# A four-block graph network on one core: transfers ordered by stream, an empty instruction as holder of TensorE's waits, and new stage orders

## The chip, the cores and the metric

The kernel runs on one core of one Trainium2 chip. The metric is the device time of one execution in microseconds, the median of a few runs. The text uses the names of the profile for the engines: PE (TensorE), DVE (VectorE), ACT (ScalarE), POOL (GpSimd) and SP (SyncE, which here does nothing but wait and issue transfers); PEld is the loading of weights into PE.

## The reference, cut to what matters

128 graphs of 64 nodes with 384 features pass four blocks. Each block takes h = relu(layernorm(x)), computes f(h) and adds it to x, all in float32.

```python
h = jnp.maximum(_layernorm(x, axis=-1), 0.0)
x = x + _L0_gnn_ref(h, adj, ...)      # two layers, attention from two projections of h
h = jnp.maximum(_layernorm(x, axis=-1), 0.0)
x = x + _L1_gnn_ref(h, adj, adj, ...) # 12-head attention, bias adj + adj
h = jnp.maximum(_layernorm(x, axis=-1), 0.0)
x = x + _L2_gnn_ref(h, adj, ...)      # 12-head attention, bias adj
h = jnp.maximum(_layernorm(x, axis=-1), 0.0)
x = x + _L3_gnn_ref(h, adj, ...)      # two layers, upper, diagonal and lower part apart
```

One layer of the first block, and of the last:

```python
u = u_left * adj_tri + u_left * diag_mask + u_right * jnp.swapaxes(adj_tri, 1, 2)
delta_exp_u = jnp.exp(u) * adj
attention = delta_exp_u / (jnp.sum(delta_exp_u, axis=2, keepdims=True) + 1e-10)
ctx = jnp.matmul(attention, h @ W_lin.T + b_lin)
h = jax.nn.relu(_layer_norm(ctx, ln_a[l], ln_b[l]))
...
ctx = jnp.einsum('bij,bjd->bid', attn * upper, hl) + diag_a[..., None] * hs + jnp.einsum('bij,bjd->bid', attn * lower, hr)
```

## The kernel before, in words

**Tiles.** A group is 4 graphs, 256 rows of x, held as 128 partitions by 2 by 384. There are 32 groups. They are dealt to two streams, 0 and 1, with buffers and four PSUM banks each; a stream does 16 groups (ITER) per block. The blocks (phases) run one after the other with a barrier between them: phase 0 is the first block, phases 1 and 2 are the attention blocks, phase 3 the last. x goes to memory between phases.

**Products.** A projection is done as three matmuls on a high and a low part (`exact_product`, L161 to L163). `ml`, `mr` and `lin` are the three projections of a layer in phase 0, `w0`, `w1`, `w2` those in phase 3, `q`, `k`, `v`, `out` those of attention. PE's transposes (`hT`, `pt`, `aT`) and the small products (`u` or `scores`, `agg` or `pv`) stand between them.

**Order.** Each phase has four lists of words, one for each of PE, ACT, DVE and POOL (`GCN0_ORDERS`, `ATT_ORDERS`, `GCN3_ORDERS`). A word such as `agg_0.1` is a stage, its layer and its stream; a prime means that the stage works in round r on group r-1. `run_stages` issues the list once a round, rounds 2 to 15 as a loop. Each engine goes through its list in that order and waits where a count of another engine is not yet reached; nothing overtakes. So a list fixes what stands behind a stage that waits.

**A group's way.** SP brings x (`xin`) and the adjacency (`adjin`); DVE takes row statistics (`stat`), POOL makes scale and shift of them (`stat` on POOL, four small operations, one of them a power), ACT makes h (`norm`, L432, L828, L1230), PE transposes it (`hT`), ACT and DVE split it in high and low part (`t_lo` is the last), and the projections follow. In a layer, `ea` is the masked exponential, `aT` its transpose, `lin` or `w2` on DVE the evacuation of a projection with its bias, which `agg` on PE reads. In attention, DVE's `soft` and `fac` give a factor by which POOL's `p` scales the exponentials (three pieces p0, p1, p2), PE transposes them (`pt0` to `pt2`), ACT evacuates (`pT`), PE multiplies by v (`pv0` to `pv2`).

**Transfers.** SP's program is `move_program`. In a round it waits and issues for stream 0 and stream 1 the loads of group i, and then for stream 0 and stream 1 the stores of group i-1 (with `x_again`, a second load of x for the residual, in phases 0 and 3). A load waits until the buffers are free: `adjin` by a stage of POOL, `xin` by ACT's `norm`. A store waits for DVE's `xout`. SP is one queue too: a load behind a store waits for that store's wait.

**A small matmul that waits.** Before `agg` and `pv`, PE issues `take_wait` (L121): a product of the identity with one column, into a corner of a PSUM bank that nobody reads. The waits of the stage are on it, and the tiled matmuls after it wait for nothing.

Of the kernel before, what the change touches and what calls it, by code (L numbers as in the profile page):

```python
# [12 lines left out]
STREAMS = 2  # L13
GROUPS = GRAPHS * NODES // TOK
ITER = GROUPS // STREAMS
HEADS = 12
HD = FEAT // HEADS
HT = HEADS * T
HPC = P // HD
BANK = 512  # L20
# [8 lines left out]
GCN0_ORDERS = [  # L29
# [10 lines left out]
]  # L40
PT_BANK = (0, 2, 3)
ATT_ORDERS = [
# [6 lines left out]
]  # L49
GCN3_ORDERS = [  # L50
# [13 lines left out]
]  # L64
# [53 lines left out]

def take_wait(nc, g, b, bank=1):

    nc.tensor.matmul(b.ps[0:HD, bank, BANK - 1:BANK], g.ident[:, 0:HD], g.ident[:, 0:1], start=True, stop=True)  # L121

# [82 lines left out]
def move_program(nc, sp, g, phase, n_mats, rows, x_out, bufs, sems, adj_free, x_free, x_new,  # L205
                 x_again=None):
# [15 lines left out]
    def store(s, i):  # L222
        x_new(s, i)
        sp.dma_start(x_out[i * STREAMS + s], bufs[s].xout[:]).then_inc(sems.stored[s], 16)
# [17 lines left out]

    def turn(i):
        for s in range(STREAMS):
            load(s, i, i - 1)
        for s in range(STREAMS):
            store(s, i - 1)
            if x_again:
                x_again(s, i)
    turn(1)  # L250
    with sp.Fori(2, ITER) as i:
        turn(i)
    if phase + 1 < len(g.sources):
        for s in range(STREAMS):
            sp.wait_ge(sems.stored[s], 16 * (ITER - 1) + 1)
            load(s, 0, ITER - 1, of=phase + 1)
    for s in range(STREAMS):
        store(s, ITER - 1)
    for s in range(STREAMS):
# [28 lines left out]
def gcn0_phase(nc, g, phase, x_out, b_lin, gain, beta, ln_cols):  # L288
# [20 lines left out]
    with ExitStack() as ctx:  # L309
        def sb(name, shape, dt=F32):  # L310
            return ctx.enter_context(nc.sbuf_tensor(f"{name}_{phase}", shape, dt))
        sems = phase_sems(nc, g, ctx, phase)
# [8 lines left out]
        for s in range(STREAMS):  # L321
            b = Buf()
# [291 lines left out]
        def _(pe):  # L614
            pe.wait_ge(g.const_in, g.const_count)

            def layer(l):
# [62 lines left out]
                def agg(s, i):  # L680
                    b = bufs[s]

                    pe.wait_ge(dve_done[s], DV[s](f"lin_{l}", i))
                    pe.wait_ge(act_done[s], AC[s](f"aT_{l}", i))
                    take_wait(nc, g, b, 2 * l + 1)
                    for half in range(2):
# [13 lines left out]
def attention_phase(nc, g, phase, bias_times, x_out, bv, bo):  # L700
# [13 lines left out]
    with ExitStack() as ctx:  # L714
        def sb(name, shape, dt=F32):
            return ctx.enter_context(nc.sbuf_tensor(f"{name}_{phase}", shape, dt))
        sems = phase_sems(nc, g, ctx, phase)
# [5 lines left out]
        for s in range(STREAMS):  # L723
            b = Buf()
# [231 lines left out]
        def _(pe):  # L956
# [66 lines left out]
            def pv(c):  # L1023
                def stage(s, i):
                    b = bufs[s]
                    pe.wait_ge(act_done[s], AC[s](f"pt{c}", i))
                    take_wait(nc, g, b)
                    for t in range(T):
# [29 lines left out]
def gcn3_phase(nc, g, phase, x_out, w_rows, gain, beta, ln_cols):  # L1058
# [19 lines left out]
    with ExitStack() as ctx:  # L1078
# [353 lines left out]
        def _(pe):  # L1432
            pe.wait_ge(g.const_in, g.const_count)

            def layer(l):
# [61 lines left out]
                def agg(s, i):  # L1497
# [3 lines left out]
                    pe.wait_ge(pool_done[s], PO[s](f"w0_{l}", i))  # L1501
                    take_wait(nc, g, b, 3)
                    for k, m in enumerate((UPPER, LOWER)):
# [128 lines left out]
```

## Time and profile before

| | |
|---|---|
| median of three runs | 3173.35 us (3173.3 to 3178.01) |
| the profiled execution, its own time | 3173.94 us |
| its span, first to last instruction | 3172.1 us |
| PE busy | 2881.0 us, 91% |
| DVE, POOL, ACT busy | 2047.8, 1251.3, 1215.9 us |
| transfers | 158.83 MB, mean 50 GB/s |

The profiled execution lies 0.6 us above the median, and 1.8 us of its time are outside the span. In the profile a line of a view is a group of instructions or a stretch of time; "idle ... <- X" is time in which the engine had nothing running, with the instruction whose end released it.
### The profile page before, as it was taken

Reading aid. Unit: us, or ns where it says so; the run is one execution under the profiler, and the core shown is the slowest. Engines: PE = TensorE matmul, PEld = TensorE weight load, DVE = VectorE, ACT = ScalarE, POOL = GpSimd, SP = SyncE. Lnnn points to the kernel's source line nnn. Section 1 sums busy time; section 2 is a strip of 40 time slices with the busy share of each in tenths; the row PEclk is TensorE's granted clock in tenths of the full one; section 3 lists DMA queues with packets and bytes.
Section 4 is the critical chain, followed back from the end, with each engine's and each line's share of the span. In section 5 each row is a group of like instructions: output and inputs, shape, how many; then the busy total and the mean of one; then the engine's idle time right before and its main releaser. Section 6 shows DMA issues by size and latency. Waiting matters only on the chain. (4 is left out here: it accounts for less than half of the span.)

```text
span 3172.1 us, 83110 instructions
## 1 busy us (share of the span) xinstructions
PE 2881.0 (91%) x33408; PEld 2633.1 (83%) x33408; DVE 2047.8 (65%) x3932; ACT 1215.9 (38%) x1941; POOL 1251.3 (39%) x2315
## 2 busy tenths in 40 slices
PE   6999999999978999999969999999699999999997
PEld 6888888888877888888858888888588888888886
DVE  4655665656665777777657777777566666666666
ACT  3333333333333333333333333333344444444443
POOL 2111211212113333333323333333267777676767
PEclk9999999999999999999989999999799999999999
DMA  3111111111111111111111111111201010111010
GB/s 132 48 54 45 46 63 45 38 63 46 63 47 59 44 43 43 43 44 44 47 57 45 43 48 43 43 43 43 74 14 67 33 66 33 66 33 66 33 65 31
DMA packets 116483, 158.83 MB, mean 50 GB/s; under 512 B 8000, under 2 KB 112320, under 8 KB 116416
## 3 DMA queue, kind: packets, MB, share of 16 engines
q1 hardware_dynamic: 116416, 157.88, 15.2%
q8 instruction: 49, 0.80, 0.1%
q14 instruction: 18, 0.15, 0.0%
HBM read 107.52 MB, written 50.33 MB: 50 GB/s over the span
## 5 line engine op out<-in xcount | busy, mean ns | idle before, releaser
L161 PE MATMUL ps<-t_hi,w_hi 128*128 128x256 f32 x2304 | 669.6, 291 | 44.9 <-DVE t_lo L898 42.3
L162 PE MATMUL ps<-t_lo,w_hi 128*128 128x256 f32 x2304 | 652.6, 283 | 0.0
L163 PE MATMUL ps<-t_hi,w_lo 128*128 128x256 f32 x2304 | 651.7, 283 | 0.0
L161 PE MATMUL ps<-w_hi,t_hi 128*128 128x384 f32 x1536 | 532.9, 347 | 16.2 <-DVE t_lo L1348 12.4
L163 PE MATMUL ps<-w_hi,t_lo 128*128 128x384 f32 x1536 | 518.1, 337 | 0.0
L162 PE MATMUL ps<-w_lo,t_hi 128*128 128x384 f32 x1536 | 518.0, 337 | 0.0
L161 PEld LDWEIGHTS ps<-t_hi,w_hi 128*128 128x128 f32 x2304 | 442.8, 192 | 75.3 <-DVE t_lo L898 52.1
L812 POOL TENSOR_TENSOR e<-e,factor 128x512 f32<-128x512 f32 x192 | 195.3, 1046 | 762.9 <-DVE factor L936 762.9
L162 PEld LDWEIGHTS ps<-t_lo,w_hi 128*128 128x128 f32 x2304 | 442.8, 192 | 0.0
L163 PEld LDWEIGHTS ps<-t_hi,w_lo 128*128 128x128 f32 x2304 | 441.6, 192 | 0.0
L161 PEld LDWEIGHTS ps<-w_hi,t_hi 128*128 128x128 f32 x1536 | 288.4, 188 | 28.6 <-DVE t_lo L1348 14.4
L1194 POOL TENSOR_TENSOR hw<-hw,w_row 128x192 f32<-128x192 f32 x512 | 294.7, 610 | 39.2 <-ACT hw L1275 39.0
L162 PEld LDWEIGHTS ps<-w_lo,t_hi 128*128 128x128 f32 x1536 | 288.9, 188 | 0.0
L163 PEld LDWEIGHTS ps<-w_hi,t_lo 128*128 128x128 f32 x1536 | 288.4, 188 | 0.0
L415 POOL TENSOR_TENSOR rstd<-mv,pos_half 128x2 f32<-128x2 f32 x64 | 44.1, 690 | 577.8 <-DVE mv L592 577.8
L942 DVE TENSOR_TENSOR o_lo<-ps,o_hi 128x768 fp32r<-128x768 f32 x64 | 61.3, 958 | 294.9 <-ACT o_hi L867 294.9
L848 ACT ACTIVATE k<-ps 128x768 f32<-128x768 f32 x64 | 52.0, 813 | 397.5 <-PE ps L163 397.5
L1275 ACT ACTIVATE hw<-ps 128x768 f32<-128x768 f32 x128 | 103.6, 810 | 205.4 <-PE ps L163 205.4
L843 ACT ACTIVATE q<-ps 128x768 f32<-128x768 f32 x64 | 52.1, 814 | 291.0 <-PE ps L163 291.0
L804 POOL TENSOR_TENSOR xout<-xin,bo_row 128x192 f32<-128x192 f32 x256 | 143.7, 595 | 0.0
L161 PE MATMUL ps<-w_hi,o_hi 128*128 128x384 f32 x384 | 131.9, 343 | 4.7 <-DVE o_lo L942 4.7
L161 PE MATMUL ps<-w_hi,swap_hi 128*128 128x384 f32 x384 | 134.4, 350 | 0.0
(152 smaller groups left out, 6165.6 us busy)
## 6 DMA issues: line engine op xcount, KB each, us to landing
x_after<-xout SPq DMA_DIRECT2D x96, 384.0 KB, 2.5
xin<-x_after SPq DMA_DIRECT2D x96, 384.0 KB, 3.4
xin<-in_x SPq DMA_DIRECT2D x32, 384.0 KB, 4.7
x<-in_x SPq DMA_DIRECT2D x32, 384.0 KB, 3.6
x<-x_after SPq DMA_DIRECT2D x32, 384.0 KB, 4.2
out<-xout SPq DMA_DIRECT2D x32, 384.0 KB, 3.0
w_raw<-in_w SPq DMA_DIRECT2D x4, 2304.0 KB, 9.3
adjin<-in_adj SPq DMA_DIRECT2D x32, 256.0 KB, 4.3
```

The source lines that it names most:

```text
L161: nc.tensor.matmul(out, lhs_hi, rhs_hi, start=(k == 0), stop=False)
L162: nc.tensor.matmul(out, lhs_hi, rhs_lo, start=False, stop=False)
L163: last = nc.tensor.matmul(out, lhs_lo, rhs_hi, start=False, stop=(k == len(terms) - 1))
L415: nc.gpsimd.tensor_tensor(b.rstd[:], b.mv[:, :, 1], g.pos_half[:, 0:T], ALU.pow).then_inc(pool_done[s], 1)
L804: ins = nc.gpsimd.tensor_tensor(b.xout[:, rows, at], b.xin[:, rows, at], bo_row[:, at], ALU.add)
L812: nc.gpsimd.tensor_tensor(b.e_rows[:, c * n:(c + 1) * n], b.e_rows[:, c * n:(c + 1) * n], b.factor[:, c * n:(c + 1) * n].unsqueeze(2).broa ...
L843: nc.scalar.activation(b.q[:], b.ps_row, ACT.Copy).then_inc(act_done[s], 1)
L848: nc.scalar.activation(b.k[:], b.ps_row2, ACT.Copy).then_inc(act_done[s], 1)
L942: nc.vector.tensor_tensor(b.o_lo_by_graph, b.ps_o, b.o_hi_by_graph.bitcast(F32), ALU.subtract)\
L1194: ins = nc.gpsimd.tensor_tensor(b.hw[:, rows, m, at], b.hw[:, rows, m, at], w_row[l][m][:, at], ALU.add)
L1275: nc.scalar.activation(b.hw[:, :, m], b.ps_w[m], ACT.Copy).then_inc(act_done[s], 1)
```

## The change

Three things are changed; what is computed is the same.

1. `move_program`: the loop goes by stream. For each stream it stores group i-2, loads x again for group i-1, and loads group i. At the end of a phase the first load of the next phase stands by its stream, and waits for one store less.
2. `take_wait` with its matmul becomes `take_waits`, which issues `nop` on PE. In the built program it is a bare wait of PE's sequencer; no matmul stands there.
3. All twelve orders are new. In phases 0 and 3 they also start at another place of the cycle, so that other stages carry the prime.

```diff
-def take_wait(nc, g, b, bank=1):
-
-    nc.tensor.matmul(b.ps[0:HD, bank, BANK - 1:BANK], g.ident[:, 0:HD], g.ident[:, 0:1], start=True, stop=True)
+def take_waits(pe):
+
+    pe.nop(nofuse=True)
...
-    def turn(i):
+    def store_and_reload(s, i):
+        store(s, i)
+        if x_again and (not isinstance(i, int) or i + 1 < ITER):
+            x_again(s, i + 1)
+    for s in range(STREAMS):
+        load(s, 1, 0)
+    with sp.Fori(2, ITER) as i:
         for s in range(STREAMS):
+            store_and_reload(s, i - 2)
             load(s, i, i - 1)
-        for s in range(STREAMS):
-            store(s, i - 1)
-            if x_again:
-                x_again(s, i)
-    turn(1)
-    with sp.Fori(2, ITER) as i:
-        turn(i)
-    if phase + 1 < len(g.sources):
-        for s in range(STREAMS):
-            sp.wait_ge(sems.stored[s], 16 * (ITER - 1) + 1)
+    for s in range(STREAMS):
+        store_and_reload(s, ITER - 2)
+        if phase + 1 < len(g.sources):
+            sp.wait_ge(sems.stored[s], 16 * (ITER - 2) + 1)
             load(s, 0, ITER - 1, of=phase + 1)
     for s in range(STREAMS):
-        store(s, ITER - 1)
+        store_and_reload(s, ITER - 1)
...
-                    take_wait(nc, g, b, 2 * l + 1)
+                    take_waits(pe)
```

Of the orders, PE's list of phase 0 and DVE's of attention:

```diff
-    "ml_1.0' agg_0.1' mr_1.0' u_1.0' hT_1.1' lin_1.0' aT_1.0' mr_1.1' agg_1.0' hT_0.0 ml_1.1' ml_0.0 "
-    "mr_0.0 u_1.1' lin_1.1' aT_1.1' u_0.0 hT_0.1 lin_0.0 aT_0.0 agg_1.1' agg_0.0 ml_0.1 mr_0.1 hT_1.0 "
-    "u_0.1 lin_0.1 aT_0.1",
+    "aT_1.0' mr_1.1' hT_0.0 agg_1.0' u_1.1' lin_1.1' mr_0.0 aT_1.1' ml_0.0 hT_0.1 u_0.0 lin_0.0 aT_0.0 "
+    "agg_1.1' agg_0.0 ml_0.1 mr_0.1 hT_1.0 u_0.1 lin_0.1 aT_0.1 agg_0.1 ml_1.0 mr_1.0 hT_1.1 lin_1.0 "
+    "u_1.0 ml_1.1",
...
-    "stat.0 pv.0' hT.0 soft.1' out.0' fac.1' v.0 stat.1 pv.1' hT.1 soft.0 out.1' fac.0 v.1",
+    "stat.0 pv.0' hT.0 soft.1' out.0' stat.1 fac.1' v.0 pv.1' hT.1 soft.0 out.1' fac.0 v.1",
```

**SP in the loop of phase 0.** The rows are in order of issue; the number at the end of `xin0`, `xout0_0` is the stream. Before:

```order
30 L216 DMA adjin0<-in_adj 128x512
31 L361 ISA
32 L220 ISA
33 L220 DMA xin0<-in_x 128x2x384
34 L358 ISA
35 L216 ISA
36 L216 DMA adjin1<-in_adj 128x512
37 L361 REGISTER_ALU
38 L220 ISA
39 L220 DMA xin1<-in_x 128x2x384
40 L364 ISA
41 L224 ISA
```

The stores (L224) come behind both loads, and the next round's loads behind both stores. Now:

```order
26 L225 DMA x_after_0<-xout0_0 128x2x384
27 L369 ISA
28 L369 DMA x0_0<-in_x 128x2x384
29 L360 ISA
30 L217 ISA
31 L217 DMA adjin0<-in_adj 128x512
32 L363 REGISTER_ALU
33 L221 ISA
34 L221 DMA xin0<-in_x 128x2x384
35 L366 REGISTER_ALU
36 L225 ISA
37 L225 DMA x_after_0<-xout1_0 128x2x384
```

The load of stream 0 now stands right behind the store of stream 0, and ahead of that of stream 1.

**DVE in the loop of attention, stream 1's softmax.** `sum`, `rsum`, `factor` are the stage `fac`; `x_st1`, `x_mv1` are stream 1's row statistics. Before:

```order
343 L949 TENSOR_TENSOR xout0_1<-ps0,xout0_1 128x768
344 L930 REGISTER_ALU
345 L931 TENSOR_REDUCE sum1_1<-e1_1 128x24
346 L879 REGISTER_ALU
347 L933 RECIPROCAL rsum1_1<-sum1_1 128x24
348 L879 REGISTER_ALU
349 L936 SCALAR_TENSOR_TENSOR factor1_1<-absmax1_1,rsum1_1 128x24
350 L906 REGISTER_ALU
351 L907 TENSOR_TENSOR v0_1<-ps0,bv_row_1 128x768
352 L885 BN_STATS x_st1_1<-xin1 128x6 x2
353 L888 MEMSET pad 128x1
354 L890 BN_AGGR x_mv1_1<-x_st1_1 128x2 x2
```

Now:

```order
341 L951 TENSOR_TENSOR xout0_1<-ps0,xout0_1 128x768
342 L887 BN_STATS x_st1_1<-xin1 128x6 x2
343 L881 REGISTER_ALU
344 L890 MEMSET pad 128x1
345 L892 BN_AGGR x_mv1_1<-x_st1_1 128x2 x2
346 L932 REGISTER_ALU
347 L933 TENSOR_REDUCE sum1_1<-e1_1 128x24
348 L881 REGISTER_ALU
349 L935 RECIPROCAL rsum1_1<-sum1_1 128x24
350 L938 SCALAR_TENSOR_TENSOR factor1_1<-absmax1_1,rsum1_1 128x24
```

The statistics of stream 1 moved ahead of the factor. On ACT `norm.1` moved with them, from behind the evacuations `pt0.1'` to `pt2.1'` to ahead of `k.0`; stream 0's stages kept their places on both engines but for `pt2.0'`, which now goes before `pt1.0'`.

## Rows read from the trace of the kernel before

**Rows 1.** The page: the span, and each engine's busy time.

```profile
span 3172.1 us, 83110 instructions
PE 2881.0 (91%) x33408; PEld 2633.1 (83%) x33408; DVE 2047.8 (65%) x3932; ACT 1215.9 (38%) x1941; POOL 1251.3 (39%) x2315
```

**Rows 2.** Windows: us, busy time by engine, granted clock; two rounds of phase 0.

```profile
523.20:581.50 58.30, 54.30 (x454) 49.30 (x453) 34.37 (x88) 19.34 (x37) 10.53 (x24) 0.97 0.15 49
...
637.40:693.30 55.90, 52.79 (x454) 47.79 (x453) 34.38 (x88) 19.30 (x37) 10.53 (x24) 1.00 0.16 52
```

**Rows 3.** PE's waits, 118 to 918 us (phase 0): total, times, longest.

```profile
PE ps L668 <- ACT mlr L465: 16.0, 28, 0.9
PE ps L627 <- ACT h L432: 15.1, 14, 1.1
PE ps L121 <- DVE hw L553: 13.1, 14, 1.6
PE ps L677 <- DVE ea L571: 3.8, 14, 0.3
```

**Rows 4.** The same, 1020 to 1560 us (phase 1).

```profile
PE ps L965 <- ACT h L828: 22.0, 27, 1.4
PE ps L161 <- DVE t_lo L898: 16.1, 27, 0.7
```

**Rows 5.** The same, 2390 to 3120 us (phase 3).

```profile
PE ps L161 <- DVE t_lo L1348: 11.5, 13, 0.9
PE ps L121 <- DVE aT L1392: 7.7, 13, 0.6
PE ps L1447 <- ACT h L1230: 6.1, 12, 0.9
```

**Rows 6.** Timeline of SP and DVE, phase 0: start, us, what, idle before.

```profile
521.75 0.40 SPq L224 DMA_DIRECT2D x_after<-xout  x1
...
523.84 0.37 SPq L220 DMA_DIRECT2D xin<-in_x  x1
...
528.87 1.02 DVE L503 BATCH_NORM_STATS2 x_st<-xin 128x6 f32<-128x384 f32 x2 [2.77 <-DMA xin<-in_x]
```

**Rows 7.** Timeline of PE, phase 0: a round's cluster of waits, and one in its end.

```profile
531.15 0.22 PE L121 MATMUL ps<-ident 128*32 128x1 f32 x2 [1.45 <-DVE hw L553]
...
533.25 1.24 PE L627 MATMUL ps<-ident,h 128*128 128x128 f32 x6 [1.07 <-ACT h L432]
...
937.06 0.22 PE L121 MATMUL ps<-ident 128*32 128x1 f32 x2 [0.94 <-DVE hw L553]
```

**Rows 8.** Timeline of SP and DVE in phase 1.

```profile
1299.53 0.40 SPq L220 DMA_DIRECT2D xin<-x_after  x1
...
1302.90 1.02 DVE L885 BATCH_NORM_STATS2 x_st<-xin 128x6 f32<-128x384 f32 x2 [2.06 <-DMA xin<-x_after]
```

**Rows 9.** Timeline of PE, ACT and POOL in phase 1, stream 0's half.

```profile
1300.05 3.05 POOL L812 TENSOR_TENSOR e<-e,factor 128x512 f32<-128x512 f32 x3 [12.15 <-DVE factor L936]
...
1302.74 1.47 PE L1019 MATMUL ps<-ident,e 128*128 128x128 f32 x12
...
1303.64 1.57 ACT L859 ACTIVATE pT<-ps 128x512 f32<-128x512 f32 x3
1305.84 1.30 ACT L828 ACTIVATE h<-xin,x_shift,x_rstd 128x384 f32<-128x384 f32 x2 [0.62 <-POOL x_shift L786]
...
1304.82 0.22 PE L121 MATMUL ps<-ident 128*32 128x1 f32 x2
1304.98 0.45 PE L1033 MATMUL ps<-pT,v 64*32 64x64 f32 x32
...
1307.20 0.88 PE L965 MATMUL ps<-ident,h 128*128 128x128 f32 x6 [1.23 <-ACT h L828]
```

**Rows 10.** Lines: the waiting matmul's group; PEld behind a wait held by a register instruction.

```profile
L121 PE MATMUL ps<-ident 128*32 128x1 f32 x640 | 71.3, 181 | 30.9 <-DVE hw L553 15.0 <-DVE aT L1392 9.3 <-DVE hw L1357 1.0
...
1308.00 0.62 PEld L1007 LDWEIGHTS ps<-k,q 32*64 32x64 f32 x49 [0.17 <-issue]
```

More of the change, by code:

```diff
@@ L1026, in stage @@
                     pe.wait_ge(act_done[s], AC[s](f"pt{c}", i))
-                    take_wait(nc, g, b)
+                    take_waits(pe)
                     for t in range(T):
@@ L1501, in agg @@
                     pe.wait_ge(pool_done[s], PO[s](f"w0_{l}", i))
-                    take_wait(nc, g, b, 3)
+                    take_waits(pe)
                     for k, m in enumerate((UPPER, LOWER)):
```

51 rows, old and new, of tables (ATT_ORDERS, GCN0_ORDERS, GCN3_ORDERS) are left out of this document.

## The prediction, made before the changed kernel ran

> **What bounds the kernel now.** The page comes first: PE is busy 2881.0 of 3172.1 us, DVE as the next only 2047.8 [rows 1]. So an edit is worth what it takes out of PE's queue or out of its waits. Next I read PE's waits phase by phase, in stretches of whole rounds away from the phase ends. Phase 0: 48.0 us in 14 rounds, 3.4 a round [rows 3]. Phase 1: 38.1 us in 13.7 rounds of 39.4 us, 2.8 a round [rows 4], and phase 2 has the same program. Phase 3: 25.3 us in 13.5 rounds of 54.2 us, 1.9 a round [rows 5]. Together they are some 160 us, and that is about what orders can win. The releasers are always the last link of a chain over DVE and ACT (t_lo, h, mlr, hw).
>
> Two things in the windows and timelines make some of these waits longer than the chain needs.
>
> First, x comes late. In phase 0 SP issues the load of stream 0 at 523.84, after the store of stream 1 at 521.75, and DVE, whose `stat.0` stands ahead of `lin_1.1'`, sits idle 2.77 us for it [rows 6]. Behind that `stat` PE waits 1.45 us for hw and then 1.07 us for h [rows 7]. In phase 1 the same load is issued at 1299.53 and DVE idles 2.06 us [rows 8]; h then starts 0.6 us after ACT's last pT [rows 9] and PE waits 1.23 us for it, against 0.48 us in stream 1's half.
>
> Second, the clock. A round of phase 0 takes 58.3 us at granted clock 0.97, with PE busy 54.30 us, and 55.9 us at 1.00, with 52.79 us for the same 454 matmuls [rows 2]. In the first, after the 1.45 and 1.07 us of waiting, the transpose takes 1.24 us [rows 7]: PE fell from 2.4 to 1.2 GHz there. Of the 14 rounds 8 are of that kind.
>
> **The transfers.** In SP's new loop the load of stream 0 stands behind the store of stream 0 alone. In phase 0 that store is issued half a round before stream 1's, and the load then waits for POOL to have read `adjin`, which happens before stream 1's xout in the new order too. So x is there some 10 us or more before `stat.0`, and the 2.77 us are gone. Stream 1's load is queued behind the wait for stream 1's xout as before, but its `stat` stands later behind that point on all lists. The extra queueing (a store now waits behind the other stream's load) costs nothing: the load's waits end before the xout it stands ahead of. In phase 1 the load can go when POOL's `xb.0` and `bias.0` are done, 10 us before 1299.53.
>
> **Attention, per round.** Stream 0's half: x no longer late, DVE's `stat.0` ends about 1302.2 rather than 1304.2. POOL finishes p at 1303.10 (1300.05 plus 3.05), its four stat operations take about 1.6 us, so shift is there at 1304.7 and h can start when ACT has done the third pT, at 1305.2, rather than at 1305.84 [rows 9]. That is 0.6 us. Stream 1's half: `norm.1` leaves the place behind pT, so h (1.30 us) is off the chain and the transpose can follow `pv2` at once. But `stat.1` now delays the factor by 1.02 plus 0.33 us. POOL's pieces come at 1.02 us each; PE had 1.6 us of slack on p0 (1301.1 against 1302.74 [rows 9]), and the third piece will now be some 0.65 us late. And what is late next is o_hi on ACT and t_lo on DVE, which start only 0.2 to 0.3 us earlier. I take 0.2 us. Together 0.8 us a round, times 15 rounds, times 2 phases: **24 us**. If the third piece is later than I think, stream 1's half loses 0.4 us instead: 0.2 us a round is the low end, 6 us.
>
> **Phase 0, per round.** I followed PE's new list through the round with the durations of the rows and these gaps between engines, stage by stage. The h wait (1.07) and the hw wait of `agg_1.1'` (0.55 to 1.45) go, as `stat.0` and `lin_1.1'` lie well ahead of their readers. `u_1.1'` gets `hT_0.0` and `agg_1.0'` ahead of it and finds mlr ready, and `u_1.0` has `lin_1.0` ahead. That takes the 0.9 us one away. What stays or comes: `u_0.0` and `u_0.1` have only one transpose between them and the projection that they need, which shows as 0.24 us each in rounds of before (28 waits hold 16.0 us, in pairs of 0.90 and 0.24 [rows 3]). And `agg_0.1` now stands right behind `aT_0.1` and `lin_0.1`, without `ml_1.0` between them: it waits for DVE to evacuate hw. The trace has that very sequence in the tail of the phase: 0.94 us [rows 7]. With 0.1 us for a tight `aT_0.0` that is 1.5 us in place of 3.4. So 1.9 us a round.
>
> **The empty instruction.** The small matmul comes 320 times (640 records, two each [rows 10]). From its start to the first tiled matmul go 0.16 us (1304.82 to 1304.98 [rows 9]), 51 us in all. In attention the first two of three stand in a stretch that ACT's pT sets (three in 1.57 us, and PE's three repeat at the same 0.53 us), so only the last counts, and I have it in the 0.2 us. In phases 0 and 3 there are four a round on PE's path. No row shows a bare wait ahead of these tiles. The nearest is the wait that a register instruction holds ahead of `scores`: PEld pauses 0.17 us there [rows 10] while PE runs on. So each stop is worth between +0.16 (all of it) and -0.17 us (the pause falls on PE too). Most waits of `agg` are over before PE arrives, so I take the near side: 0.1 us, 0.4 us a round.
>
> The Trainium skill ("PSUM — Partial Sum Buffer", Engine vs sequencer instructions) counts a nop among the instructions that the sequencer runs itself, while weight loads overlap running matmuls inside the engine. By that rule the tiles' weight loads could not be taken up before the wait ends. No row shows it for `agg`; it is the low side of the bound above, and the sum stands without it.
>
> Phase 0 is then 2.3 us times 15 rounds, 35 us. The cluster of waits that came before the fall of the clock is gone, so I count the 1.5 us of 8 rounds too: 12 us. **47 us**.
>
> **Phase 3, per round.** h loses its late x, `w0` gets other work ahead, and aT's evacuation too. By the walk `agg_0.0` and `agg_0.1` wait for DVE's w2, which stands behind splits and `stat`-like work: 0.5 us each as a gap, about 0.35 as the profile counts it. So 0.7 in place of 1.9 us; with the empty instruction 1.2 plus 0.4, times 15: **24 us**. One place could fail here: `adj_1.1'` is now primed, so stream 1's load goes out only in the new round. It should land 2 us before `stat.1` wants it.
>
> **Phase ends.** The tails hold the same stages as before in nearly the same order, and at the start of a phase x was there already; I count 0.
>
> **Sum.** 24 + 47 + 24 = 95 us off 3173.9, the execution's own time: **3079 us**, and 3078 for a median such as that shown.
>
> **The rivals.**
>
> *Only the transfers pay.* The walk fixes no wait that I didn't look for; DVE runs in order, and one stage placed ahead of its input gives each gain back. Then what stays is what the late x cost: 0.6 us in 30 attention rounds (18), about 1.0 us in 15 rounds of phase 0 (15), the clock (12), and 0.4 in phase 3 (6): 51 us, 3123. For it: the new order of phase 0 has slack below 1 us at four places. Against it: I found those slacks positive. If the loads, against what SP's list says, still come late because POOL frees `adjin` late, it is the reverse: 95 less 45, 3129.
>
> *More than the sum.* Attention also ran below full clock (0.98 on average in phase 1); without falls there and with the full 0.16 us for the stops: another 15 and 10 us, 3054.
>
> *The bare wait costs.* At -0.17 us on all 320 stops the sum loses 54 us and the 12 counted: 3145. By the page's rule above it would go that way.
>
> *Slower: the clock.* The new 0.94 us wait with short ones about it could put PE at 1.2 GHz in every round, where now most of the run is at 2.4. At 1.5 us a fall, once a round in phases 0 and 3 (32) and once in each half round of attention (64): 144 us, plus the 12 counted, from 3079: 3235. It decides the sign from 63 falls on. For it: rows 2 show falls after waits. Against: they came where two waits of over 1 us lay 2 us apart [rows 7], and no such pair is left; attention with waits of 1.23 us has few falls.
>
> **How the numbers follow.** Forecast 0.58 (3055 to 3105); only the transfers, or the loads late, 0.19 (3123, 3129); more than the sum 0.12 (3054 and less); the bare wait 0.06 (3145); slower 0.05 (3235). I choose the range 3040 to 3132: it leaves out the last two cases and the far end of the third. What a measurement can tell from no change is about 0.2%, 6 us. Faster by more than that 0.93, within it 0.02, slower 0.05.
>
> **What would show it.** In the changed profile: no DVE idle on `xin` in the rounds; SP's load of stream 0 alone, far from stream 1's; h waits of PE near 0.6 us in one half of attention and near none in the other; one hw wait of about 0.9 us a round in phase 0; rounds of about 53.8, 38.5 and 52.6 us in the three kinds of phase; granted clock 1.00 in nearly all of phase 0. The forecast is wrong if `stat.1` ahead of `fac.1'` makes PE wait for POOL's e by more than 1 us, if `agg` and `pv` start late behind their bare waits, or if new waits of over 1 us stand close together.

## The result, and the profile after

| | before | changed |
|---|---|---|
| median of four runs, same chip | 3175.68 us (3173.3 to 3179.95) | 3056.23 us (3054.35 to 3056.87) |
| ratio, 95% interval | | 0.9621 (0.9605 to 0.9638) |
| the profiled execution, its own time | 3173.94 us | 3056.15 us |
| its span | 3172.1 us | 3054.4 us |

The change takes 117.7 us off the span where 95 were forecast. The page of the changed kernel, in the form of [rows 1]; its third line is the granted clock in 40 slices, in tenths:

```profile
span 3054.4 us, 82121 instructions
PE 2807.4 (92%) x32768; PEld 2576.5 (84%) x32768; DVE 2043.4 (67%) x3932; ACT 1214.8 (40%) x1941; POOL 1311.5 (43%) x2315
...
PEclk9999999999989999999989999999799999999999
```

PE still sets the time. Its busy time fell by 73.6 us and its idle time (span less busy) by 44.1 us, from 291.1 to 247.0. Of the busy time 46.9 us went with the 640 small matmuls and 26.7 us from matmuls that both kernels have; the run with transfers and orders alone, below, parts the two.

The four phases of both kernels follow, each row from the start of a phase to the start of the next: length, busy time of PE, PEld, DVE, ACT and POOL with counts, granted clock, share of the DMA engines, GB/s. First before:

```profile
0.00:948.60 948.60, 860.97 (x7232) 780.49 (x7232) 557.16 (x1416) 317.40 (x584) 172.29 (x394) 0.98 0.17 57
948.60:1613.10 664.50, 593.09 (x9792) 559.10 (x9792) 449.98 (x518) 239.72 (x325) 224.81 (x386) 0.96 0.14 46
1613.10:2272.60 659.50, 585.71 (x9792) 552.54 (x9792) 449.22 (x518) 239.71 (x325) 224.77 (x385) 0.97 0.15 46
2272.60:3172.10 899.50, 841.26 (x6592) 740.98 (x6592) 591.41 (x1480) 419.03 (x710) 629.40 (x1152) 0.98 0.15 49
```

And the changed kernel:

```profile
0.00:894.70 894.70, 829.33 (x7104) 756.37 (x7104) 547.04 (x1419) 315.61 (x584) 189.94 (x394) 0.99 0.18 61
894.70:1539.30 644.60, 575.79 (x9600) 543.14 (x9600) 445.72 (x521) 241.98 (x325) 224.14 (x386) 0.98 0.15 47
1539.30:2183.80 644.50, 577.40 (x9600) 544.51 (x9600) 445.75 (x518) 241.80 (x325) 224.03 (x385) 0.97 0.15 47
2183.80:3054.40 870.60, 824.85 (x6464) 732.51 (x6464) 604.88 (x1480) 415.38 (x710) 673.43 (x1152) 0.98 0.16 50
```

The gains are 53.9, 19.9, 15.0 and 28.9 us; the forecast had 47, 12, 12 and 24. A round of phase 0 in the form of [rows 2], and one of phase 3:

```profile
474.27:527.77 53.50, 51.56 (x446) 47.05 (x445) 33.67 (x89) 19.22 (x36) 11.80 (x24) 1.00 0.16 54
...
2381.61:2433.94 52.33, 51.25 (x406) 45.50 (x405) 37.50 (x93) 25.57 (x45) 42.14 (x73) 1.00 0.16 50
```

PE's waits (total, times, longest) in phase 0, 110 to 900 us, in the form of [rows 3]:

```profile
PE ps L692 <- DVE hw L555: 17.4, 15, 1.5
PE ps L692 <- DVE asum L578: 4.4, 14, 0.3
PE ps L670 <- ACT mlr L467: 3.4, 14, 0.2
PE ps L670 <- ACT mlr L462: 3.4, 14, 0.2
```

in phase 1, 920 to 1514 us, in the form of [rows 4]:

```profile
PE ps L162 <- DVE t_lo L900: 23.0, 30, 0.8
PE ps L1035 <- ACT pT L861: 8.4, 17, 0.5
PE ps L1021 <- POOL e L814: 6.3, 17, 0.9
PE ps L967 <- ACT h L830: 3.6, 15, 0.2
```

and in phase 3, 2250 to 3000 us, all that is left of the kinds of [rows 5]:

```profile
PE ps L1510 <- DVE hw L1359: 14.7, 29, 0.7
```

SP in phase 0, where [rows 6] had the load of stream 0 2.1 us behind the store of stream 1. Now the load of stream 0 stands 17.8 us ahead of that store (493.95), and no round shows DVE idle on `xin`:

```profile
474.27 0.40 SPq L225 DMA_DIRECT2D x_after<-xout  x1
...
476.14 0.38 SPq L221 DMA_DIRECT2D xin<-in_x  x1
493.95 0.40 SPq L225 DMA_DIRECT2D x_after<-xout  x1
```

### The profile page after: what moved, and what is told of

Read it like the earlier page. It is cut to its first block and busy times, and to the rows that moved or that the text cites. A ratio compares the mean times of both kernels' runs of the same rounds, so it can differ in the third digit from the quotient of the medians.

```text
span 3054.4 us, 82121 instructions
## 1 busy us (share of the span) xinstructions
PE 2807.4 (92%) x32768; PEld 2576.5 (84%) x32768; DVE 2043.4 (67%) x3932; ACT 1214.8 (40%) x1941; POOL 1311.5 (43%) x2315
## 5 line engine op out<-in xcount | busy, mean ns | idle before, releaser
L162 PE MATMUL ps<-t_hi,w_hi 128*128 128x256 f32 x2304 | 662.7, 288 | 51.7 <-DVE t_lo L900 49.1
L1196 POOL TENSOR_TENSOR hw<-hw,w_row 128x192 f32<-128x192 f32 x512 | 348.1, 711 | 53.8 <-ACT hw L1277 52.3
L417 POOL TENSOR_TENSOR rstd<-mv,pos_half 128x2 f32<-128x2 f32 x64 | 53.4, 835 | 459.9 <-DVE mv L594 459.9
L781 POOL TENSOR_TENSOR x_shift<-x_mv,neg_one 128x2 f32<-128x2 f32 x64 | 14.3, 224 | 351.0 <-DVE x_mv L892 351.0
L544 DVE CAST t_hi<-hT 128x768 fp32r<-128x768 f32 x64 | 35.7, 558 | 191.6 <-ACT hT L446 137.2
```

Source lines behind the costliest of these rows:

```text
L162: nc.tensor.matmul(out, lhs_hi, rhs_hi, start=(k == 0), stop=False)
L417: nc.gpsimd.tensor_tensor(b.rstd[:], b.mv[:, :, 1], g.pos_half[:, 0:T], ALU.pow).then_inc(pool_done[s], 1)
L1196: ins = nc.gpsimd.tensor_tensor(b.hw[:, rows, m, at], b.hw[:, rows, m, at], w_row[l][m][:, at], ALU.add)
```

## The experiments

The theory is that of the prediction: the loads come in time, the orders take waits away, and each stop is a little shorter. The rivals are that the transfers alone pay, that a bare wait costs, and that the orders are worth something without the early loads. Each of the three parts was made alone and with each other one; four runs then undo or alter single moves, one sizes the stop, and one repeats the changed kernel. None leaves out any part of the reference. A ratio stands against runs of the kernel before on the same chip beside it. Spans and phases are of one profiled execution each.

| | median us | ratio (95%) | span | phase 0, 1, 2, 3 |
|---|---|---|---|---|
| before | | | 3172.1 | 948.6, 664.5, 659.5, 899.5 |
| transfers alone | 3097.23 | 0.9779 (0.9763 to 0.9796) | 3094.2 | 905.0, 649.2, 649.2, 890.8 |
| stops alone | 3158.86 | 0.9971 (0.996 to 0.9981) | 3154.1 | 938.0, 661.7, 659.5, 894.9 |
| orders alone | 3260.94 | 1.0294 (1.0277 to 1.0311) | 3259.8 | 985.9, 664.2, 662.7, 947.0 |
| transfers and orders | 3082.34 | 0.9732 (0.9716 to 0.9749) | 3080.9 | 900.4, 651.0, 652.0, 877.5 |
| orders and stops | 3247.33 | 1.0251 (1.0221 to 1.028) | 3247.1 | 982.7, 658.4, 656.9, 949.1 |
| transfers and stops | 3084.66 | 0.972 (0.9699 to 0.9741) | 3083.3 | 898.5, 649.0, 651.2, 884.6 |
| all three | 3056.23 | 0.9621 (0.9605 to 0.9638) | 3054.4 | 894.7, 644.6, 644.5, 870.6 |

The kernel before took 3163.1 to 3180.0 us over all its executions, so a span set against its 3172.1 is less sure than the ratio. By the medians on one chip the transfers alone are worth 71.6 us (77.9 by span), the stops alone 9.9 (18.0), and the orders alone cost 92.2 (87.7). With the new transfers the repeats of a kernel lie within 6 us of each other.

### Transfers alone (e1_transfers)

The kernel before with the new SP loop:

```diff
-    def turn(i):
-        for s in range(STREAMS):
-            load(s, i, i - 1)
-        for s in range(STREAMS):
-            store(s, i - 1)
...
+    with sp.Fori(2, ITER) as i:
+        for s in range(STREAMS):
+            store_and_reload(s, i - 2)
+            load(s, i, i - 1)
```

> The kernel before with the new transfer program alone; old orders and the small waiting matmul stay. Theory (late x costs waits and, through them, clock): DVE's idle of 2.8 us on xin in phase 0 is gone, h comes earlier in phase 0 and in stream 0's half of attention, and the falls of the clock in phase 0 go. 51 us off 3175.7, so about 3125 (3110 to 3145). Rival (the orders carry the gain, x could be late without cost): at most 10 us off, 3166 or more.

Measured: 3097.23 us, faster than the expected range. That is 71.6 us by the medians and 77.9 us off the span, where I had sized 51. The phases of this kernel:

```profile
0.00:905.00 905.00, 845.68 (x7232) 767.13 (x7232) 556.44 (x1416) 317.15 (x584) 170.84 (x394) 1.00 0.18 60
905.00:1554.20 649.20, 583.99 (x9792) 551.43 (x9792) 447.83 (x519) 237.95 (x325) 223.86 (x386) 0.98 0.15 47
1554.20:2203.40 649.20, 584.73 (x9792) 552.13 (x9792) 447.70 (x519) 237.84 (x325) 223.77 (x385) 0.98 0.15 47
2203.40:3094.20 890.80, 840.07 (x6592) 742.96 (x6592) 590.56 (x1480) 418.15 (x710) 631.43 (x1152) 0.98 0.15 49
```

and PE's waits in phase 0, 25 to 880 us:

```profile
PE ps L669 <- ACT mlr L466: 19.2, 33, 0.9
...
PE ps L121 <- DVE hw L554: 0.9, 1, 0.9
```

In phase 0 both kinds of wait that follow stream 0's `stat` are gone, h and hw, 28.2 us in 14 rounds [rows 3], not the h wait alone. The idle time falls from 87.6 to 59.3 us and, for the same 7232 matmuls, the busy time from 860.97 to 845.68 at a granted clock of 1.00 for 0.98. Over the four phases 51.3 us are idle time and 26.6 us busy time.

### The empty instruction alone (e2_nop)

```diff
-    nc.tensor.matmul(b.ps[0:HD, bank, BANK - 1:BANK], g.ident[:, 0:HD], g.ident[:, 0:1], start=True, stop=True)
+    pe.nop(nofuse=True)
```

> The kernel before with the empty instruction alone in place of the small waiting matmul. Theory (each stop saves 0.06 us where its wait ends last and 0.15 us where it is over already): 10 to 20 us off, about 3160 (3153 to 3168). Rival (a bare wait holds back the weight loads and costs about what the matmul cost): 3176, up to 3230 at 0.17 us lost per stop.

Measured: 0.9971, 9.9 us between the medians, the low end of the 10 to 20 expected. The two profiled spans lie 18.0 us apart, 10.6 of it in phase 0 and 4.6 in phase 3. In these two executions the small matmuls' own busy time goes (43.2 us), and 25.2 us come back as idle time: where the stop waits for something, shortening it only starts the wait earlier. A bare wait does not cost, so that rival falls.

### The orders alone (e3_orders), and orders and empty instruction on the old transfers (e5_old_transfers)

The first is the kernel before with all twelve new lists, of which PE's list of phase 0 shows the kind:

```diff
-    "ml_1.0' agg_0.1' mr_1.0' u_1.0' hT_1.1' lin_1.0' aT_1.0' mr_1.1' agg_1.0' hT_0.0 ml_1.1' ml_0.0 "
+    "aT_1.0' mr_1.1' hT_0.0 agg_1.0' u_1.1' lin_1.1' mr_0.0 aT_1.1' ml_0.0 hT_0.1 u_0.0 lin_0.0 aT_0.0 "
```

> The kernel before with the new orders alone; old transfers and the small waiting matmul stay. Theory (the new orders take stat.0 soon after stream 1's xout, and count on x being there): stream 0's x lands 7 us after the store of stream 1, DVE stands still for some 5 us a round, PE's h wait grows by 3 to 4 us a round in phases 0 and 3 and 0.6 in attention; nothing is left of the gain: about 3186 (3160 to 3210). Rival (the three parts add up, and the orders carry most): 3115 or less.

The second is the changed kernel with the old SP loop:

```diff
-            store_and_reload(s, i - 2)
...
+        for s in range(STREAMS):
+            store(s, i - 1)
+            if x_again:
+                x_again(s, i)
+    turn(1)
```

> The changed kernel with the old transfer program. Theory (new orders need the early x): DVE stands still on xin for several us a round, and PE's wait for h comes to 3 us or more a round in phases 0 and 3: about 3170 (3145 to 3195). Rival (transfers and orders add up, transfers 51 us): 3107.

Measured: 3260.94 and 3247.33 us, both slower than the kernel before, some 75 us above the theory's value for each and above both ranges. Phases 0 and 3 of the second, and its waits there (25 to 958 and 2323 to 3222 us):

```profile
0.00:982.70 982.70, 862.16 (x7104) 775.42 (x7104) 549.61 (x1417) 318.19 (x584) 189.58 (x394) 0.96 0.17 55
...
2298.00:3247.10 949.10, 852.55 (x6464) 762.87 (x6464) 592.87 (x1480) 412.23 (x710) 670.20 (x1152) 0.94 0.15 46
```

```profile
PE ps L628 <- ACT h L433: 54.9, 14, 5.6
```

```profile
PE ps L162 <- DVE t_lo L1349: 51.4, 14, 4.2
```

and, in the timeline of a round of phase 0, the statistics with the idle time ahead of them and the transpose of h behind:

```profile
604.86 1.02 DVE L504 BATCH_NORM_STATS2 x_st<-xin 128x6 f32<-128x384 f32 x2 [3.71 <-DMA xin<-in_x]
...
609.14 1.37 PE L628 MATMUL ps<-ident,h 128*128 128x128 f32 x6 [3.46 <-ACT h L433]
610.44 1.56 PE L691 MATMUL ps<-hw,aT 64*64 64x384 f32 x8
```

The wait is of the size that I had given, 3.9 us a round in phase 0 (54.9 by 14). What the expectation lacked is the clock. After the wait the transposes take 1.37 us and the tiles of `agg` 1.56 us; in the changed kernel they take 0.82 and 0.88 us. Against the changed kernel, with the same 7104 and 6464 matmuls, PE is busy 32.8 us longer in phase 0 and 27.7 us in phase 3, 60.5 us of the 77 that the value for the second was off. The new orders place `hT_0.0` and what follows it early in the round. With the old loads they are not a small gain but a loss of 87.7 us of span.

### Transfers and orders, with the small matmul (e4_no_nop)

```diff
-                    take_waits(pe)
+                    take_wait(nc, g, b, 2 * l + 1)
```

> The changed kernel with the small waiting matmul put back. Theory: 15 us slower than the changed kernel, about 3071 (3064 to 3078). Rival (bare waits cost as much as the matmul): 3056 or less.

Measured: 3082.34 us, above the 3064 to 3078 expected. The empty instruction is worth 26.5 us in the changed kernel, not 12: 5.7 in phase 0 and 6.9 in phase 3, as counted (6 each), but also 6.4 and 7.5 in the two attention phases, where I had given it nothing of its own. This kernel has the 33,408 matmuls of the kernel before, so the two compare phase by phase:

```profile
0.00:900.40 900.40, 840.12 (x7232) 765.30 (x7232) 546.69 (x1416) 316.43 (x584) 190.39 (x394) 0.99 0.18 60
900.40:1551.40 651.00, 591.14 (x9792) 553.07 (x9792) 444.60 (x519) 243.24 (x325) 224.04 (x386) 0.97 0.14 47
1551.40:2203.40 652.00, 588.11 (x9792) 550.19 (x9792) 444.43 (x521) 243.45 (x325) 223.94 (x386) 0.98 0.15 47
2203.40:3080.90 877.50, 834.97 (x6592) 738.92 (x6592) 607.62 (x1480) 415.33 (x710) 672.37 (x1152) 0.98 0.16 50
```

The stop itself, in the same sequence with nothing to wait for. First this kernel, then the changed one:

```profile
503.98 0.82 PE L629 MATMUL ps<-ident,h 128*128 128x128 f32 x6
504.73 0.22 PE L122 MATMUL ps<-ident 128*32 128x1 f32 x2
504.88 0.55 PE L692 MATMUL ps<-hw,aT 64*64 64x384 f32 x4
```

```profile
500.87 0.82 PE L629 MATMUL ps<-ident,h 128*128 128x128 f32 x6
501.62 0.55 PE L692 MATMUL ps<-hw,aT 64*64 64x384 f32 x4
```

From the transposes to the first tile it is 0.90 us with the small matmul and 0.75 without: the stop costs nothing that can be seen. And where hw is late, first before, then changed:

```profile
643.43 0.93 DVE L553 TENSOR_TENSOR hw<-ps,lin_row 128x768 f32<-128x768 f32 x1
...
644.49 0.22 PE L121 MATMUL ps<-ident 128*32 128x1 f32 x2 [0.55 <-DVE hw L553]
644.63 0.55 PE L690 MATMUL ps<-hw,aT 64*64 64x384 f32 x4
```

```profile
480.42 0.96 DVE L555 TENSOR_TENSOR hw<-ps,lin_row 128x768 f32<-128x768 f32 x1 [0.16 <-PE ps L164]
...
481.63 0.88 PE L692 MATMUL ps<-hw,aT 64*64 64x384 f32 x8 [1.14 <-DVE hw L555]
```

From hw's end to the first tile it is 0.27 us (644.36 to 644.63) and 0.25 us (481.38 to 481.63). The stop is worth 0.15 us where PE comes late and 0.02 us where PE waits.

The Trainium skill ("PSUM — Partial Sum Buffer", Engine vs sequencer instructions) has the nop run by the sequencer, with weight loads overlapping inside the engine. The low side of my bound, tiles held up by 0.17 us [rows 10], to which that would fit, is not seen in these rows.

### Transfers and empty instruction, old orders (e9_old_orders)

The changed kernel with the twelve lists of before; DVE's list of attention:

```diff
-    "stat.0 pv.0' hT.0 soft.1' out.0' stat.1 fac.1' v.0 pv.1' hT.1 soft.0 out.1' fac.0 v.1",
+    "stat.0 pv.0' hT.0 soft.1' out.0' fac.1' v.0 stat.1 pv.1' hT.1 soft.0 out.1' fac.0 v.1",
```

> The changed kernel with all old orders (new transfers and the empty instruction stay). Theory (given early x and bare waits, the new orders are worth 1.2 us a round in phase 3, some 0.7 in phase 0, little in attention): about 3083 (3075 to 3090), 25 to 30 us behind the changed kernel. Rival (the orders alone carry as much as the transfers): 3110 or more.

Measured: 3084.66 us, as expected. With the early loads in place the orders alone bring 13.3 us of span, the empty instruction alone 10.9, and both 39.8. The surplus is 15.6 us (13.5 us by the medians), and attention has all of it, 15.7 us: there the one alone changes a phase by +0.2 and -2.0 us, the other by -1.8 and -2.8 (both lose a little or nothing), and together they give 4.6 and 4.7. PE's waits in phase 1, first with the transfers alone (930 to 1529 us), then with the empty instruction too (923 to 1522 us):

```profile
PE ps L966 <- ACT h L829: 14.4, 30, 0.5
```

```profile
PE ps L966 <- ACT h L829: 21.2, 31, 2.1
...
PE ps L1034 <- ACT pT L860: 5.1, 30, 0.2
```

With the old orders h comes behind the last pT on ACT. PE's shorter stops are paid back at the h wait (14.4 to 21.2 us) and at pT (5.1 us, new). In the new orders `norm.1` has left that place, the h wait is 3.6 us, and the shorter stop reaches the end of the round. What is late next is t_lo, at 23.0 us.

### Two small matmuls for one (e10_two_matmuls)

Transfers and orders, and in `take_wait`:

```diff
-    nc.tensor.matmul(b.ps[0:HD, bank, BANK - 1:BANK], g.ident[:, 0:HD], g.ident[:, 0:1], start=True, stop=True)
+    for _ in range(2):
+        nc.tensor.matmul(b.ps[0:HD, bank, BANK - 1:BANK], g.ident[:, 0:HD], g.ident[:, 0:1], start=True, stop=True)
```

> The changed kernel with two small matmuls in a row at each of the 320 stops instead of the empty instruction. Theory (a small matmul costs 0.15 us on PE where its wait is over, and delays what waits for the tiles where it isn't): the second costs as much as the first, so some 26 us more than the kernel with one, about 3108 (3100 to 3120). Rival (the first cost something that is not its run time, such as held back weight loads): 3085.

Measured: 3094.49 us, 11.6 us of span over the kernel with one; half of what the theory gave, below its range and above the rival's 3085. A row shows why:

```profile
505.21 0.29 PE L123 MATMUL ps<-ident 128*32 128x1 f32 x4
505.43 0.55 PE L693 MATMUL ps<-hw,aT 64*64 64x384 f32 x4
```

From the stop to the first tile it is 0.22 us, 0.07 more than with one. The first small matmul costs twice the second. The 26.5 us of the empty instruction are thus 320 stops at 0.08 us each, and a second small matmul adds 0.04. How the tiles would do with their waits on themselves, with no holder at all, was not tried and stays open.

### agg_0.1 moved back behind ml_1.0 (e7_agg_back)

```diff
-    "agg_1.1' agg_0.0 ml_0.1 mr_0.1 hT_1.0 u_0.1 lin_0.1 aT_0.1 agg_0.1 ml_1.0 mr_1.0 hT_1.1 lin_1.0 "
+    "agg_1.1' agg_0.0 ml_0.1 mr_0.1 hT_1.0 u_0.1 lin_0.1 aT_0.1 ml_1.0 agg_0.1 mr_1.0 hT_1.1 lin_1.0 "
```

> The changed kernel with agg_0.1 moved back behind ml_1.0 on PE in phase 0, so that DVE's hw is ready when PE comes to it. Theory (the 1.1 us wait is the price for n_0.1 in time for hT_1.1; moved back, hT_1.1 waits 1.8 us instead): 0.5 us a round slower, about 3065 (3058 to 3074). Rival (the wait is a plain loss): 1.1 us a round less, 3038.

Measured: 3072.56 us, within the range but at twice the price that I had given, phase 0 912.3 for 894.7 us. PE's costliest wait in phase 0, 25 to 887 us:

```profile
PE ps L629 <- DVE z L606: 30.4, 16, 2.0
```

The 1.16 us that PE waits for hw in each round (17.4 by 15) is a price paid on purpose. With `ml_1.0` in between, that wait is gone, and the transposes of layer 1, whose input is the output of this very `agg`, come 1.9 us late instead (30.4 by 16). Filling the hw wait loses 17.6 us in the phase, 1.1 us a round where 0.5 was expected.

### The moves in attention (e8_stat1_back, e6_att_old, e11_pt_in_order)

First the changed kernel with `stat.1` and `norm.1` where they stood before:

```diff
-    "exp.0' k.1' pt0.0' pt2.0' pt1.0' norm.0 pv.0' hT.0 q.0 exp.1' norm.1 k.0 pt0.1' pt1.1' pt2.1' pv.1' "
+    "exp.0' k.1' pt0.0' pt2.0' pt1.0' norm.0 pv.0' hT.0 q.0 exp.1' k.0 pt0.1' pt1.1' pt2.1' norm.1 pv.1' "
...
-    "stat.0 xb.1' bias.1' stat.1 p.1' xb.0 bias.0 p.0",
+    "stat.0 xb.1' bias.1' p.1' stat.1 xb.0 bias.0 p.0",
```

> The changed kernel with stream 1's statistics and norm back behind its factor in attention (DVE, POOL and ACT), nothing else. Theory (0.2 to 0.3 us a round of stream 1's half came from this move): 6 to 9 us slower than the changed kernel, 3064 (3058 to 3070). Rival (stat.1 ahead of the factor makes p late and costs what it gives): 3056 or less.

Then the changed kernel with all four old lists of attention, among them:

```diff
-    "k.1' pt0.0' pt2.0' pt1.0' pv0.0' pv1.0' pv2.0' hT.0 scores.1' q.0 out.0' v.0 k.0 pt0.1' pt1.1' "
-    "pt2.1' pv0.1' pv1.1' pv2.1' hT.1 scores.0 q.1 out.1' v.1",
+    "v.1' k.1' pt0.0' pt1.0' pt2.0' pv0.0' pv1.0' pv2.0' hT.0 scores.1' q.0 out.0' v.0 k.0 pt0.1' pt1.1' "
+    "pt2.1' pv0.1' pv1.1' pv2.1' hT.1 scores.0 q.1 out.1'",
```

> The changed kernel with the old orders in attention alone. Theory (in attention the early x gave 0.6 us a round by itself, the orders the rest of 1.1 us): 12 us slower than the changed kernel, about 3068 (3062 to 3076). Rival (there the orders did nothing, or all): 3056, or 3090.

And the changed kernel with only the swap of stream 0's pieces taken back, on PE and ACT:

```diff
-    "k.1' pt0.0' pt2.0' pt1.0' pv0.0' pv1.0' pv2.0' hT.0 scores.1' q.0 out.0' v.0 k.0 pt0.1' pt1.1' "
+    "k.1' pt0.0' pt1.0' pt2.0' pv0.0' pv1.0' pv2.0' hT.0 scores.1' q.0 out.0' v.0 k.0 pt0.1' pt1.1' "
```

> The changed kernel with stream 0's transposes pt0, pt1, pt2 in number order again on PE and ACT. Theory (POOL's three pieces are ready, h ends last after pv): within 3 us of the changed kernel. Rival (pv1 ready early lets pv follow piece by piece, 0.1 us a round and more): 3 to 8 us faster.

| | median us | ratio (95%) | span | phase 0, 1, 2, 3 |
|---|---|---|---|---|
| stat.1 and norm.1 back | 3068.06 | 0.9684 (0.9663 to 0.9705) | 3065.9 | 894.5, 651.3, 648.8, 871.3 |
| all attention orders old | 3061.26 | 0.9663 (0.9643 to 0.9684) | 3060.0 | 895.1, 647.9, 650.3, 866.7 |
| pieces in order | 3054.54 | 0.9632 (0.9611 to 0.9653) | 3052.0 | 894.4, 642.0, 644.7, 870.9 |

Moving the two stages back costs 11.0 us in the two attention phases, and the old lists altogether 9.1. So the whole gain of the new attention orders is in that one move. By the medians the old lists cost only 5.0 us, below the 12 of the theory and just outside its range, and the one move back 11.8: without that move the other new places in the lists gain nothing and may lose. PE's waits with it undone, phase 1, 920 to 1521 us:

```profile
PE ps L967 <- ACT h L830: 15.1, 31, 2.1
PE ps L1035 <- ACT pT L861: 10.8, 31, 0.5
```

The h wait is back at 15.1 us for 3.6, while pT and e fall a little (11.6 us for 14.7 in sum). The swap of the pieces is worth nothing: the kernel without it differs from the changed one by 1.7 us with overlapping intervals. It is no better version, and none of the others beats the changed kernel. With all attention orders old phase 3 is 3.9 us shorter, though its lists weren't touched. Two of its rounds take 104.2 us (from one store of SP to another, 2443.13 to 2547.32), for 104.7 in the changed kernel (2433.94 to 2538.60), and why stays open. So a difference of some 4 us in a phase need not come from the lists of that phase.

### The changed kernel again (e12_changed_again)

No line is edited.

> The changed kernel once more, beside the other three on one chip, as their base: 3050 to 3058.

Measured: 3056.72 us, ratio 0.9636 (0.9617 to 0.9656), phases 894.9, 644.1, 645.3 and 871.1 us. The repeat is within 0.8 us in each phase.

## Why the prediction was right, and where its sum was off

The sign and the range were right, and so was the mechanism in the main: early loads, fewer waits, cheaper stops. The time was 23 us lower than forecast, and the parts did not share the gain as the walk had it. Because transfers and orders with the small matmul keep all matmuls of the kernel before, the 117.7 us fall into three parts that answer to the parts of the sum: idle time between the two (291.1 to 226.6), busy time of the same matmuls (2881.0 to 2854.3), and the empty instruction on top.

| term | forecast us | measured us |
|---|---|---|
| waits of PE, phase 0 | 28 (1.9 a round) | 27.3 |
| waits, attention | 24 | 11.5 + 9.9 |
| waits, phase 3 | 18 (1.2 a round) | 15.7 |
| empty instruction | 12 (phases 0 and 3 alone) | 26.5 (5.7, 6.4, 7.5, 6.9) |
| busy time of the same matmuls, phase 0 (forecast as clock) | 12 | 20.9, of which 15.3 with the transfers alone |
| the same, other phases | 0 | 5.8 (1.9, -2.4, 6.3) |

**The waits of PE held.** Phase 0, stage by stage: one hw wait a round, foretold 0.94 from the tail of the phase, came at 1.16 (17.4 by 15); the pair of 0.24 at u came at 0.24 each (3.4 by 14, twice); the tight `aT_0.0` foretold at 0.1 is the asum wait of 0.31. These make 1.95 us a round for the 1.5 foretold; the 27.3 us of the table are measured with the small matmul in place, where no asum wait shows. A round lasts 53.5 us in phase 0, 38.2 in attention (one of SP's stores of phase 1 to the next, 1004.38 to 1042.58) and 52.3 in phase 3, for 53.8, 38.5 and 52.6 foretold. In attention the h wait fell to 0.24 us in one half and to none in the other, where 0.6 and near none were foretold. In phase 3 the two agg waits are 0.51 each (14.7 by 29), for 0.35 foretold. All three sums are within 3 us. Of the signs that would have spoken against the forecast none came: the longest wait for POOL's e is 0.9 us, and the bare waits start nothing late. "What is late next is o_hi on ACT and t_lo on DVE" named the right limit: t_lo went from 18.1 us (31 waits, before, 974 to 1588 us) to 23.0.

**The empty instruction was mis-sized.** The step that failed is "only the last counts, and I have it in the 0.2 us": it gave the stops of attention nothing of their own, and they brought 13.9 us. The reason given, that two of the three stand in a stretch set by ACT's pT, held for the old orders, where the empty instruction alone changes attention by next to nothing. It fails once h is off the chain.

**The clock came as sized; more busy time went than the clock's.** Before, the 8 rounds at 0.97 (117.8 to 581.5 us) hold 434.5 us of busy time, and the next 5 at 1.00 hold 264.0, or 52.8 a round: 12.1 us for the clock, as "I count the 1.5 us of 8 rounds too: 12 us" had it. With the transfers alone the whole phase gives 15.3. The other 5.6 of the 20.9 came with the new orders, at a granted clock no higher: three rounds of the same matmuls take 158.0 us of busy time with the transfers alone (386.99 to 549.43) and 157.1 with the orders too (389.18 to 551.00), all at 1.00. The forecast had no term for that, and in phase 3, at 0.98 in all three, it is 5.1 of the 6.3 us. Why the busy time falls there was not tested. In attention I had kept 15 us for the rival; busy time gave 10.1 with the transfers alone (9.1 and 1.0), and next to none with the orders beside them (1.9 and -2.4).

**The transfers carry most of it.** Alone they give 77.9 us of span, 71.6 by the medians, of which the rival "only the transfers pay" had priced 51. Its weak term was "about 1.0 us in 15 rounds of phase 0 (15)": it gave the late x the h wait alone, while my own reading had said that hw stood behind the same `stat`. The idle time of the phase fell by 28.3 us. The orders and the empty instruction then brought 39.8 us on top, for the 44 that the forecast had beyond the transfers. In phase 0 the new orders do not even lower PE's waits below those of the transfers alone. From the transfers alone to transfers and orders its idle time there goes from 59.3 to 60.3 us. The mlr waits fall from 19.2 to 8.1 us and the hw waits rise from 0.9 to 17.2 (25 to 875 us), and the orders are worth 4.6 us, all of it busy time. So the 28 us of waits came out right, but not for the reason that the walk gave: it credited a good part to the new places in the lists, and the early loads alone brought it. In phase 3 both had a part: 7.5 us of idle time went with the transfers and 8.2 more with the orders.

**Which case came.** The measured time lies nearer to the 3054 of "more than the sum" than to 3079. That case had its parts half right: the stops brought more, in attention as well; attention at full clock did not come (0.98 and 0.97 over its two phases). The stops and the busy time brought more than was counted and the waits a little less; together that makes the 23 us. One sum of the prediction is wrong as it stands: "95 less 45" is 50 us, which gives 3124 and not 3129. The case "slower by the clock" did not come in the changed kernel, but its mechanism did in the runs with the old transfers: waits of 3.3 to 5.6 us in each round, and PE busy 60.5 us longer for the same matmuls in phases 0 and 3. So single waits bring falls too when they are that long; the new hw waits of 1.16 us, one a round, left phase 0 at 0.99. The z wait in the run with `agg_0.1` moved back did not bring it down either: from 160 us on that wait is 1.9 to 2.0 us in each of 14 rounds, the six transposes behind it take 0.87 or 0.88 us, and the granted clock of that stretch is 1.00 (160 to 887 us). The kernel before fell after 1.45 and 1.07 us close together [rows 7], so a wait's length alone does not tell.

## What to carry to other kernels

Where engines run fixed lists, look at the transfer queue first: new lists that placed x's consumers early lost some 90 us with the old queue, and gained 13 with the new one, so neither can be judged alone. A shortened step that is not the last link of a chain shows nothing until that link is moved, so try the two together before dropping one as useless. And a wait of 1 us in a tight loop may be the price for a longer one later; move it alone and see before filling it.

## What the runs showed of the hardware

- A bare wait of PE's sequencer ahead of tiled matmuls delays nothing that can be seen: 0.25 us from the end of DVE's write to the first tile, 0.27 us with a small matmul as holder; 0.75 and 0.90 us from the transposes ahead when nothing is waited for.
- The first small matmul of a stop takes 0.15 us of PE's queue, a second 0.07 us.
- A late input costs PE twice: waits of 3.3 to 5.6 us came with a granted clock of 0.96 and 0.94 over phases 0 and 3, for 0.99 and 0.98 in the changed kernel, so that 106.0 us of added idle time brought 60.5 us of added busy time for the same matmuls.
- Waits of 1.9 to 2.0 us, one such in each of 14 rounds of 54.6 us, left PE at 2.4 GHz: the six transposes behind them take 0.87 or 0.88 us, and the granted clock is 1.00 from 160 to 887 us (`agg_0.1` moved back).
- Busy time can fall at an unchanged clock: three rounds of phase 0 in the old orders and in the new ones, both at 1.00, hold 158.0 and 157.1 us of it for the same matmuls.
